# Windowed attention between Mamba and feed-forward blocks: v as the stationary operand, probabilities normalised on GpSimd, PSUM banks by table

## The reference

```python
def local_attention(q, k, v):              # 8 heads of 64, windows of 64 tokens
    bq = q.reshape(b, h, w, WINDOW, d) * QK_SCALE
    bk, bv = (look_around(bk), look_around(bv))      # own window and the one before
    sim = jnp.einsum('bhwid,bhwjd->bhwij', bq, bk)
    sim = jnp.where(mask, -jnp.finfo(sim.dtype).max, sim)
    attn = jax.nn.softmax(sim, axis=-1)
    out = jnp.einsum('bhwij,bhwjd->bhwid', attn, bv)
...
for l in range(2):
    qkv = shift_token(x) @ wqkv;  q = rotary(l2norm(q) * qs);  k = rotary(l2norm(k) * ksc)
    x = x + local_attention(q, k, v) @ wo
    h = layer_norm(shift_token(x)) @ w1 + b1
    x = x + (a * gelu(g)) @ w2 + b2
```

## Time and profile before

| | |
|---|---|
| median of 3 runs | 1068.75 us (1062.86 to 1068.75) |
| span of the profiled execution | 1068.3 us, first to last instruction |
| instructions | 25986 |
| TensorE, VectorE, ScalarE, GpSimd busy | 929.2, 872.8, 786.6, 695.8 us |
| mean granted TensorE clock | 0.954 of full speed |

### The profile page before, as it was taken

One profiled execution on the slowest core, in us unless ns is written; L12 is line 12 of the kernel. 1 busy time (PEld: TensorE's weight loads), 2 busy tenths in 40 slices (PEclk: granted clock), 3 DMA queues, 4 the chain that ended last, 5 costly groups with the idle time before them and its releaser, 6 DMA issues. The chain is left out here.

```text
span 1068.3 us, 25986 instructions
## 1 busy us (share of the span) xinstructions
PE 929.2 (87%) x10152; PEld 560.7 (52%) x10152; DVE 872.8 (82%) x1244; ACT 786.6 (74%) x1897; POOL 695.8 (65%) x386
## 2 busy tenths in 40 slices
PE   5577698899889989999999989998989999987875
PEld 2223345446455565556564646465655666664463
DVE  6788987998889986999999988998898976754542
ACT  5448666886898859886999688877869877783740
POOL 3026615787588775898688859884866677763731
PEclk9788889899999989999999999999999999999986
DMA  7000100010000100000101100100000100110010
GB/s 229 11 6 10 26 1 6 17 33 9 16 16 22 38 20 25 22 24 4 35 12 26 27 13 14 31 21 17 17 22 20 27 6 17 26 27 1 21 31 11
DMA packets 22618, 25.63 MB, mean 24 GB/s; under 512 B 2869, under 2 KB 14815, under 8 KB 22495
## 3 DMA queue, kind: packets, MB, share of 16 engines
q1 hardware_dynamic: 22207, 23.81, 8.6%
q10 hardware_dynamic: 288, 0.14, 0.0%
HBM read 9.26 MB, written 2.10 MB: 11 GB/s over the span
## 5 line engine op out<-in xcount | busy, mean ns | idle before, releaser
L1062 DVE TENSOR_TENSOR_SCAN scan<-du,decay 128x1028 f32<-128x1028 f32 (+1 forms) x160 | 306.3, 1952 | 10.9 <-PE YY L1252 7.3
L768 POOL TENSOR_TENSOR rn<-ssc,expo 128x16 f32<-128x16 f32 x64 | 214.0, 3344 | 5.3
L764 POOL TENSOR_SCALAR ssc<-ss 128x16 f32<-128x16 f32 x64 | 62.4, 975 | 213.4 <-DVE ss L1119 212.8
L914 ACT ACTIVATE prob<-BB,nmax 128x128 f32<-128x128 f32 x472 | 165.7, 380 | 39.4 <-DVE nmax L1157 28.0
L859 ACT ACTIVATE decay<-delta,negA 128x1024 f32<-128x1024 f32 (+1 forms) x160 | 154.2, 986 | 18.4 <-DVE scan L1062 16.5
L773 POOL TENSOR_TENSOR qkc<-qkc,qks 128x1024 f32<-128x1024 f32 x64 | 159.6, 2493 | 2.8 <-DVE qks L1137 2.7
L1252 PE MATMUL YY<-scan,diag 64*64 64x512 f32 (+1 forms) x1280 | 143.1, 538 | 10.9 <-DVE scan L1062 10.9
L777 POOL TENSOR_TENSOR qkc<-qkc,rn 128x1024 f32<-128x1024 f32 x64 | 133.2, 2082 | 5.0
L1252 PE MATMUL AA<-wqkv,hT 128*128 128x512 f32 x256 | 128.8, 627 | 6.0 <-DVE qks L1137 3.1
L914 ACT ACTIVATION_READ_ACCUMULATOR prob<-BB,nmax 128x1 f32 x472 | 104.2, 221 | 0.0
L1119 DVE TENSOR_REDUCE ss<-sq 128x16 f32<-128x1024 f32 x64 | 77.1, 1205 | 29.6 <-ACT sq L877 29.6
(11 more groups left out here) (144 smaller groups left out, 1858.8 us busy)
## 6 DMA issues: line engine op xcount, KB each, us to landing
v_even<-v_odd SPq DMA_DIRECT2D x96, 128.0 KB, 2.3
x<-in_x SPq DMA_DIRECT2D x6, 256.0 KB, 3.4
wqkv<-in_wqkv SPq DMA_DIRECT2D x1, 1536.0 KB
xT<-in_xT SPq DMA_DIRECT2D x6, 256.0 KB, 3.0
out<-outb SPq DMA_DIRECT2D x6, 256.0 KB, 2.9
w<-in_w SPq DMA_DIRECT2D x1, 682.0 KB
xT<-in_xT SPq DMA_DIRECT2D x4, 128.0 KB, 2.6
x<-in_x SPq DMA_DIRECT2D x4, 128.0 KB, 3.5
```

The costliest lines, as they stand in the source:

```text
L768: pool.tensor_tensor(rn[:, q % 2, :], ssc[:, :], expo[:, 0:2 * HEADS], ALU.pow).then_inc(rn_sb, 1)
L914: ins = act.activation(prob[:, h, :], bank_of(q, a)[:, c * P:(c + 1) * P], ACT.Exp, bias=nmax[:, q % 2, h:h + 1], accum_out=den[:, q % 2, ...
L1062: dve.tensor_tensor_scan(state, step, a, 0.0, ALU.add, ALU.mult).then_inc(scan_sb, 1)
```

## The change

The product with v turns round. In `weighted` v is the stationary operand and `probT` moves, so the result has the channels of two heads on its partitions and the tokens along a row: the form that `attn_out` reads. `out_T` and `o_s` go, and ScalarE copies the bank straight to `oT` (`out_copy`). The factor `rden` can no longer be applied behind the product, because tokens are not rows any more; a new step `share` on GpSimd multiplies `prob` by `rden` in SBUF, and `probs_T` waits for that (`norm_sb`) and no longer for the exponentials. `prob` and `probT` have two buffers. Banks come from tables with a letter for each step and number: AA, BB or YY for the pairs, C or M for the single ones. All five orders are new. `part_b` and a buffer of the diagonals' setup share memory with other tensors.

```diff
+PAIR_TABLES = {
+    "qk_in": "ABABABBABBBABBBBABAAAAABAAABBBBBAAABAABBBABABBBBAAABAYABBBBBAYYY",
...
+    "probs_T": "BAABABBAAABABBABABABAAABBBAABBABBABBBABBBBAABABABBBBYYYBYBYBABAA",
...
+BANK_TABLES = {
...
+    "weighted": "CMCMMMCCMMCCMMMCMMCMCCCMMMMMMCCCCMMCMMMMCCCMCCMMMCMCCCCCMMCMCCCC",
...
-HOLDS = {"qk_in": "A", "qk_T": "B", "scores": "B", "probs_T": "B", "v_in": "C", "weighted": "C", "out_T": "C",
-         "attn_out": "M", "shift": "M", "norm_T": "M", "layer_T": "M", "up_gate": "AM", "up_a": "M", "down": "M"}
...
-        prob = sb("prob", [P, HEADS, P])
-        probT = sb("probT", [P, 2, HEADS, WIN])
-        o_s = sb("o_s", [P, INNER])
+        prob = sb("prob", [P, 2, HEADS, P])
+        probT = sb("probT", [P, 2, 2, HEADS, WIN])
...
+            def share(q):
+                pool.wait_ge(rden_sb, q + 1)
+                pool.tensor_tensor(prob[:, q % 2], prob[:, q % 2], rden[:, q % 2, :].unsqueeze(2).to_broadcast((P, HEADS, P)),
+                                   ALU.mult).then_inc(norm_sb, 1)
...
             def softmax(q):
-                if q:
-                    act.wait_ge(pT_ps, 2 * q)
                 if q >= 2:
-                    act.wait_ge(rden_sb, q - 1)
+                    act.wait_ge(pT_ps, 2 * (q - 1))
...
-            def out_T(q):
+            def out_copy(q):
                 l, g, i = TILE[q]
-                act.wait_ge(oT_ps, q + 1)
+                act.wait_ge(o_ps, q + 1)
...
-            def attended(q):
-                dve.wait_ge(o_ps, q + 1)
-                dve.wait_ge(rden_sb, q + 1)
-                if q:
-                    dve.wait_ge(oT_ps, q)
-                dve.tensor_tensor(heads(o_s[:, :]), heads(C[:, :]),
-                                  rden[:, q % 2, :].unsqueeze(2).to_broadcast((P, HEADS, DH)), ALU.mult).then_inc(o_sb, 1)
...
             def probs_T(q):
-                pe.wait_ge(prob_sb, 2 * q + 2)
+                pe.wait_ge(norm_sb, q + 1)
...
-                for h in range(HEADS):
-                    for wd in range(2):
-                        v = (v_even, v_odd)[wd]
-                        ins = mm(C[wd * WIN:(wd + 1) * WIN, h * DH:(h + 1) * DH],
-                                 probT[:, wd, h, :], v[:, q % V_RING, h * DH:(h + 1) * DH], h == 0, h == HEADS - 1)
+                dst = one("weighted", q)
+                for c in range(PAIRS):
+                    for w in range(2):
+                        for a in range(2):
+                            h = 2 * c + a
+                            ins = mm(dst[half(a), c * P + w * WIN:c * P + (w + 1) * WIN],
+                                     (v_even, v_odd)[w][:, q % V_RING, h * DH:(h + 1) * DH], probT[:, q % 2, w, h, :],
+                                     c == 0 and w == 0, c == PAIRS - 1 and w == 1)
...
-            def out_T(q):
-                pe.wait_ge(o_sb, q + 1)
-                free("out_T", q)
-                for c in range(INNER // P):
-                    ins = pe.transpose(C[:, c * P:(c + 1) * P], o_s[:, c * P:(c + 1) * P], ident[:, :])
-                ins.then_inc(oT_ps, 1)
```

More of the change, by code:

```diff
@@ L1189, in ffn_norm @@
                 l, g = QUAD[f]
+                rows = tiles(one("shift", f)[:, :])
                 dve.wait_ge(f_rstd, f + 1)
@@ L1290, in u_in @@
+            def free(step, *args):
+                for last, of in HELD[step, args]:
+                    pe.wait_ge(*release(last, *of))
             def u_in(g):
```

669 lines of the change are left out of this document (330 added, 339 removed).

## The result

The changed kernel takes **1130.1 us** (median of 4 runs, 1124.8 to 1132.6) beside 1065.8 for the kernel before: ratio 1.059, with a 95% interval of [1.055, 1.063]. Forecast were 1038 us and a gain of 3%.

The account below looks back on a forecast made before the run. TensorE, 94% busy in the middle, came first, with three engines close; after the change GpSimd would be fullest. From 1068.75 us, -22 + 2 - 9 + 2 - 6 + 2 = -31 gave about 1038 us, own range 1022 to 1052.

Parts of the forecast that it names:

- Part 3: Normalising on GpSimd: 543.2 us busy in the middle becomes the fullest engine; at 94.0% the middle takes 578 us, -22.
- GpSimd becomes the bound and loses: Rival: GpSimd only 87% full, the middle takes 624 us; about 1090 us in all, chance 0.12.
- Part 4: SBUF port: share and VectorE's scans exclude each other; 64 more passes make +5 us, of which +2 on the path.
- Part 1: Transposes of attended rows (41.7 us, TensorE) and o_s (43.7 us, VectorE) go; -29 in the middle if TensorE stayed the bound.
- Part 6: Banks and orders: bank pairs by table and doubled prob and probT give -6; ScalarE's five more table switches cost +2.
- Its 0 for the clock: Granted clock in the middle stays near 0.99, since TensorE stays near 90% busy there; effect 0.
- Part 2: Weighted sum with v stationary: same sixteen loads and products with roles exchanged; 0, within 7 us either way.
- the share's length: GpSimd's multiplication of 128x1024 probabilities takes as long as its existing twin product: 2.08 us each, 64 times.
- its cover: Share's chain of 7 to 9 us is hidden in the middle behind 12.7 us of TensorE work in the new order.
- signs named for a wrong forecast: TensorE waits for prob above 30 us, VectorE's for f_rs well above 8, scans over 2.6, no engine past 90% in the middle.
- Every share meets a scan: Rival: each share collides with a VectorE scan and takes 3.78 us on GpSimd; +55, about 1115 us, chance 0.03.
- Part 5: Head and tail: fewer TensorE transposes give -9; the last tiles' longer serial chain costs +2.

Follow-up runs that it names:

- a_share_behind: Changed kernel with share cut to 128x8 and, right behind it on GpSimd, a full 128x1024 pass nobody waits for: 1125.5 us, ratio 1.054.
- a_share_tiny: Changed kernel with share cut to 128x8 in place of 128x1024, same queue place and waits: 1080.5 us, ratio 1.016.
- before_twice: Kernel before, own order, with GpSimd's 128x1024 product of q and k by rn done twice per tile: 1151.8 us, ratio 1.078.
- a_no_share: Changed kernel with share taken out, the transposes waiting for the exponentials, factor 1/den left out: 1076.9 us, ratio 1.010.
- b_late_moved4: Changed code in the order of before, v stationary, without share, out_T and attended, late reciprocal, three v_in steps moved: 1056.1 us, ratio 0.990.
- before_light: Kernel before, own order and waits, with one of four transposes of attended rows and a quarter of o_s: 1052.7 us, ratio 0.986.
- before_bf16_out: Kernel before with o_s stored and transposed in bf16, and the output projection in bf16 too: 1055.8 us, ratio 0.989.
- b_share: Whole change, share included, but with the order of before and banks by kind instead of new orders and bank tables: 1351.5 us, ratio 1.266.
- b_roles_late: Changed code in the order of before, without share, out_T and attended, late reciprocal, probabilities loaded and v streamed: 1070.7 us; with v stationary 1069.5.
- the filling pass: Changed kernel with share replaced by two GpSimd memsets of 128x1024, writing SBUF and reading nothing: 1111.5 us, ratio 1.040.

## Why the prediction was wrong

**Part 3, the middle, is the step that failed.** "If the fullest engine can be as full as TensorE was (94.0%), the middle takes 543.2 / 0.940 = 578 us". The busy time in this sum was right: GpSimd is busy 547.7 us in the same work. But that work took 660 us, so GpSimd reached 83%, and no engine more than TensorE's 86%. By the same formula 83% gives 543.2 / 0.829 = 655 us, +55 for the middle; measured are +61. A pass for which nobody waits costs 45 us by its length in GpSimd's queue and by its collisions with scans (a_share_behind against a_share_tiny). Why 83% is all that it reached was not tried, and it is no limit of the engine, which stood at 87% in before_twice. GpSimd stands in a ring with VectorE (sums before, reciprocals before, scans against it) and TensorE (transposes behind); that this ring is the reason is an argument. This was the rival "GpSimd becomes the bound and loses", priced at 87% and given 0.12: its direction was right, its share of full was too high and its chance too low, and its sum had no cost of the orders. The argument against it, that GpSimd's idle time had only VectorE's lateness as a cause, counted idle time as room.

**Part 4, the port**, was right in kind and far too small. The +5 was for the long scans, which rose by 29.6 us; with the short ones it is 43.7, of which 27.7 come with the new orders alone (a_no_share) and the rest with the share. "VectorE is at 85%" did not hide them: TensorE's waits for VectorE rose from 60 to 102 us, to 94 of them already without the share.

**Part 1** had the removed work right and its worth too high: 11 to 15 us (b_late_moved4, before_light) in place of 29 in the middle, if TensorE stays the bound, and 9 outside. What took the rest stays open. VectorE is 4.6 points behind TensorE in the middle and level with it in before_bf16_out; but in b_late_moved4 VectorE is busy 36 us less than before (837.3 of 872.8), no engine is above 92% in the middle, and the gain is no larger. **Part 6** had the wrong sign: orders, banks and tables, forecast at -6 + 2, cost 21 us where no share needs them; with the share the orders save up to 221 (b_share). The orders are what keeps the share coverable, and their price belonged in the sum. Banks and orders were not parted. Its 0 for the clock did not hold either: 0.94 in the middle, and TensorE busy 921 us where 888 were forecast; what that costs by itself was not tried.

**Right were** Part 2 (v stationary costs nothing, b_roles_late), the share's length, and its cover: its place in the chain costs an estimated 5 to 10 us (a_share_behind against changed), TensorE's matmuls wait 28 us for `prob`.

Of the signs named for a wrong forecast the profile shows three: scans at 2.73 us (over 2.6), `hn` waiting 22 us for `f_rs` (8.2 in the earlier trace rows), no engine over 90% in the middle; the waits of TensorE's matmuls for `prob` stayed at 28, just under the 30 that were named, those of its weight loads were 42. The rival "Every share meets a scan" leaves out the +6 of port, tail and tables that the others have; with it, it comes to 1121.

**Part 5, head and tail**, came out near its -9 + 2 by luck: split where the middle's work begins and ends, the head grew by 13 us and the tail shrank by 19. Neither was tried apart.

**The sum as measured**, from 1067: removed work -11, orders and banks +21, share's place and waits +4, its length in GpSimd's queue +31, its reading and the rest of its length +19: 1131. Within the share's 50 us from tiny to full, TensorE's idle time grows by 27 us (174 to 202) and its busy time by 22 (899.0 to 921.4), at a clock that fell from 0.97 to 0.94 in the middle. How much of the 22 is cause and how much a consequence of the waiting was not tried. The split between length and reading is uncertain by some 5 us, since the filling pass is 0.2 us shorter and the runs with the tiny share spread over 12 us.

Against the forecast: the removed work was to bring 38 us and brought 11, a miss of 27. The share was to cost 11 (7 in the middle, from -29 to -22, then port 2 and tail 2) and cost 54, a miss of 43. Orders, banks and tables were to bring 4 and cost 21, a miss of 25.
